# Offsets' taps in four column groups, image 0's first-stage result added in the last sweep, corner rows through two banks and four tiles

## What is computed

```python
x = x + _L0_conv_ref(_gn(x), ...)   # a scan over 4096 tokens and a 3x3 convolution
x = x + _L1_conv_ref(_gn(x), ...)   # four sweeps: down, up, right, left
x = x + _L2_conv_ref(_gn(x), ...)   # column convolution times a gate
x = x + _L3_conv_ref(_gn(x), ...)   # deformable 3x3 convolution, batch norm over all images
```

```python
om = conv3x3(x, offset_w) + offset_b          # 27 channels
samp = corner(y0, x0, ..) + corner(y0, x0 + 1, ..) + corner(y0 + 1, x0, ..) + corner(y0 + 1, x0 + 1, ..)
out = einsum('bckhw,ock->bohw', samp * mask, dcn_w)
```

## Time and profile before

| | us |
|---|---|
| median of three executions | 7023.92 |
| their range | 7022.62 to 7032.38 |
| the profiled execution | 7014.16 |
| its span, first to last instruction | 7012.3 |
| PE busy in the span | 5902.3 (84%) |
| DVE busy | 5302.7 (76%) |
| POOL busy | 4107.6 (59%) |
| ACT busy | 3572.3 (51%) |

### The profile page before, as it was taken

One profiled execution on the slowest core, in us unless ns is written; L12 is line 12 of the kernel. 1 busy time (PEld: TensorE's weight loads), 2 busy tenths in 40 slices (PEclk: granted clock), 3 DMA queues, 4 the chain that ended last, 5 costly groups with the idle time before them and its releaser, 6 DMA issues. The chain is left out here.

```text
span 7012.3 us, 91346 instructions
## 1 busy us (share of the span) xinstructions
PE 5902.3 (84%) x21659; PEld 3273.6 (47%) x21659; DVE 5302.7 (76%) x12723; ACT 3572.3 (51%) x7357; POOL 4107.6 (59%) x3869
## 2 busy tenths in 40 slices
PE   5999999999998999999998877777778787777542
PEld 2444444444447888888885333333333333333221
DVE  6999999999994555566664478787878787777767
ACT  4878878788885531122221345454545454545433
POOL 4999999999991000100000277777777777777773
PEclk9999999999999999999999998989989899999765
DMA  5455444444442000000002478787878787878777
GB/s 193 169 181 184 164 170 171 171 168 169 171 164 83 3 4 0 0 0 0 0 0 67 142 237 247 230 252 223 261 219 266 210 271 211 265 220 251 224 209 288
DMA packets 325492, 1132.55 MB, mean 162 GB/s; under 512 B 58527, under 2 KB 59568, under 8 KB 283952
## 3 DMA queue, kind: packets, MB, share of 16 engines
q0 software_dynamic: 187200, 629.56, 30.3%
q1 hardware_dynamic: 137846, 498.65, 19.7%
HBM read 997.68 MB, written 130.29 MB: 161 GB/s over the span
## 5 line engine op out<-in xcount | busy, mean ns | idle before, releaser
L1255 POOL DMA_INDIRECT d_ring<-corner_table,d_idx_now x2304 | 2210.7, 960 | 925.4 <-issue 848.1
L959 POOL TENSOR_TENSOR X<-X 128x512 f32<-128x512 f32 x1024 | 1288.2, 1274 | 169.3 <-DVE X L997 153.0
L1301 ACT ACTIVATE d_mix<-d_ring,d_w_now 128x128 f32<-128x128 f32 x2304 | 735.5, 390 | 1223.2 <-DMA d_ring<-corner_table,d_idx_now 1151.4
L271 PE MATMUL prop_ps<-prop_parts,prop_w_hi 128*128 128x496 f32 (+2 forms) x4536 | 1143.2, 396 | 0.0
L997 DVE TENSOR_TENSOR_SCAN X<-X,m_pB 128x512 f32<-128x512 f32 x896 | 1135.8, 1273 | 0.0
L853 PE MATMUL m_pY<-X,small 128*128 128x512 f32 x2048 | 1040.5, 605 | 90.1 <-POOL X L959 89.9
L1623 DVE SCALAR_TENSOR_TENSOR d_acc<-d_ring,d_w_now,d_mix 128x128 f32<-128x128 f32 x2304 | 662.9, 355 | 564.2 <-ACT d_mix L1301 543.7
L1449 PE MATMUL d_ps_s<-small,d_mix 128*128 128x128 f32 x2304 | 430.3, 317 | 777.1 <-DVE d_mix L1623 775.5
L271 PEld LDWEIGHTS prop_ps<-prop_parts,prop_w_hi 128*128 128x128 f32 x4536 | 819.1, 189 | 162.3
L1449 PEld LDWEIGHTS d_ps_s<-small,d_mix 128*128 128x128 f32 x2304 | 281.3, 157 | 1276.5 <-DVE d_mix L1623 683.7
L215 ACT ACTIVATE prop_parts<-X 128x256 fp32r (+1 forms) x512 | 276.7, 541 | 1170.8 <-DVE X L292 1170.3
(11 more groups left out here) (229 smaller groups left out, 7568.9 us busy)
## 6 DMA issues: line engine op xcount, KB each, us to landing
X<-c_scratch SPq DMA_DIRECT2D x256, 1024.0 KB, 4.9
corner_table<-d_tT SPq DMA_DIRECT2D x264, 256.0 KB
d_ring<-corner_table,d_idx_now POOLq DMA_INDIRECT x2304
X<-in_x SPq DMA_DIRECT2D x8, 2048.0 KB, 15.2
m_res<-in_x SPq DMA_DIRECT2D x64, 256.0 KB, 4.6
x_scratch<-m_res SPq DMA_DIRECT2D x64, 256.0 KB, 2.1
x_scratch<-X SPq DMA_DIRECT2D x8, 2048.0 KB, 8.6
b_x<-x_scratch POOLq DMA_DIRECT2D x16, 1024.0 KB, 11.8
```

The source lines that it names most:

```text
L271: mm = pe.matmul(ps[s][:, :, :, a:b], w_hi[:, d % 2, k * P:(k + 1) * P], parts[s][:, :, :, PAD + a + k - MID:PAD + b + k - MID], start=Fal ...
L959: pool.tensor_tensor(hc[:, n % NHC, :], h[:, n, :], Cb[:, n, :], ALU.mult).then_inc(s.HC, 1)
L1255: pool.indirect_dma_start(out=ring[:, m % RING, :], out_offset=None, in_=flat, in_offset=bass.IndirectOffsetOnAxis(ap=idx_now[:, c % 2, m: ...
L1301: r0 = act.activation(R[:, k % 3, t, :], ring[:, m % RING, 0:P], ACT.Copy, scale=w_now[:, c % 2, 4 * m:4 * m + 1])
```

## The change

There are three parts.

**Offsets.** The weights of a tap are padded from 27 to 32 columns, and tap `tap` writes partitions `32 * (tap % 4)` to `32 * (tap % 4) + 31` of `ps_a`, so that the nine products are summed in four groups of 32 partitions. ACT copies all 128 partitions (the bias stands in the first 27), and the four turning matmuls take 128 rows and four identities stacked on one another, which sums the groups.

**Image 0's `x1`.** SP loads it in layer 1, whole, into 8 of the 12 tiles of `ring`, which is now allocated there. In the last sweep DVE adds a column of 64 elements of it behind each `lo` of group 0, one column late; the last is added behind the loop. In `add_x1`, image 0 keeps only the statistics. The zeroing of the second table moves to layer 1 too: POOL zeroes the 4 other tiles and issues 17 DMAs from them. In the block of layers 2 and 3, POOL has no `ring` to zero, and SP has eight loads less and one small store more.

**Corner rows.** While nothing is sampled (pass -1), round `m` uses `ps_b` or `ps_s[0]` in turn and one of four tiles, the halves of `tT` and two of `samp`; PE waits for the copy of round `m - 2`, ACT for the store of round `m - 4`. In the other passes all this stays as it was, but the semaphores of the stores are four instead of two.

```diff
@@ layer1 @@
+                sp.dma_start(first_x1[:].rearrange("p h w -> p (h w)"), x1_dram[:, 0:HW]).then_inc(G.first_x1_landed, 16)
...
+                clear = G.ring[0:W + 1, HW // (4 * P):, :]
+                pool.memset(clear.rearrange("p r e -> p (r e)"), 0.0).then_inc(s_zero, 1)
                 weights2.make(pool)
+                pool.wait_ge(s_zero, 2)
+                for x0 in range(0, W + 1, clear.shape[1]):
+                    n = min(clear.shape[1], W + 1 - x0)
+                    pool.dma_start(G.table[1, :, x0:x0 + n, :], clear[:, 0:n, :]).then_inc(G.table_cleared, 16)
...
+                def add_first_x1(t):
+                    dve.wait_ge(s_lo[0], t + (1 + H * 3))
+                    x = line(3, 0, t)[:, 0, :]
+                    dve.tensor_tensor(x, x, first_x1[:, :, t * -1 + (H - 1)], ALU.add).then_inc(s_added, 1)
...
                             rest_of_line(d, t, s)
+                            if s == 0 and d == 3:
+                                add_first_x1(t - 1)
@@ layers2_and_3 @@
-                    for i in range(NCH):
-                        sp.dma_start(first_x1(i), x1_dram[:, CH * i:CH * (i + 1)]).then_inc(s_first[i // 4], 16)
+                    sp.sem_inc(s_add, NCH)
...
-                    pool.memset(ring[:].rearrange("p r e -> p (r e)"), 0.0).then_inc(s_zero, 1)
...
+            def table_tile(s, m):
+                if s.sampling or m % TILES < 2:
+                    return tT[:, m % 2, :]
+                return samp[:, m % 2, :]
+            def table_bank(s, m):
+                return ps_b if s.sampling or m % 2 == 0 else ps_s[0]
...
-                            act.wait_ge(s_tab[m % 2], 16 * IMAGE_STORES[m % 2] * q + 16 * (m // 2))
-                            act.activation(tT[:, m % 2, :], ps_b[:].rearrange("p t c -> p (t c)"), ACT.Copy).then_inc(s_tT, 1)
+                            before = m - (2 if s.sampling else TILES)
+                            if before >= 0:
+                                act.wait_ge(s_tab[before % TILES], 16 * IMAGE_STORES[before % TILES] * q + 16 * (before // TILES + 1))
+                            act.activation(table_tile(s, m), table_bank(s, m)[:].rearrange("p t c -> p (t c)"), ACT.Copy).then_inc(s_tT, 1)
...
-                            act.activation(om_s[:], ps_a[0:NO, :], ACT.Identity, bias=off_b[:, 0:1]).then_inc(s_offs, 1)
+                            act.activation(om_s[:], ps_a[:], ACT.Identity, bias=off_b[:, 0:1]).then_inc(s_offs, 1)
...
-                        after(pe, s_tT, ROUNDS * q + m, 1)
+                        after(pe, s_tT, ROUNDS * q + m, 1 if s.sampling else 2)
...
-                        mm = pe.matmul(ps_a[0:NO, :], off_w[:, tap, :],
+                        quad = tap % QUADS
+                        mm = pe.matmul(ps_a[QUAD * quad:QUAD * (quad + 1), :], off_w[:, tap, :],
                                        xn[:, i % 2, at:at + ROWS * E].rearrange("p (h w) -> p h w", w=E)[:, :, 0:W],
-                                       start=(tap == 0), stop=(tap == TAPS - 1))
+                                       start=(tap < QUADS), stop=(tap + QUADS >= TAPS))
...
-                                turned = pe.matmul(ps_om[:, t, :], om_s[:, t * P:(t + 1) * P], G.ident[0:NO, 0:NO],
+                                turned = pe.matmul(ps_om[:, t, :], om_s[:, t * P:(t + 1) * P], off_w[:, TAPS, 0:NO],
...
-                        if isinstance(q, int) and q == 0:
-                            dve.wait_ge(s_first[i // 4], 64)
-                        else:
+                        x = XF[:, bass.ds(CH * gA, CH)]
+                        if not (isinstance(q, int) and q == 0):
                             dve.wait_ge(s_x1, 16 * gA + (16 - 16 * NCH))
-                        apart(dve, s_passed_dve)
-                        x = XF[:, bass.ds(CH * gA, CH)]
-                        dve.tensor_tensor(x, x, first_x1(i) if isinstance(q, int) and q == 0 else x1[:], ALU.add).then_inc(s_add, 1)
+                            apart(dve, s_passed_dve)
+                            dve.tensor_tensor(x, x, x1[:], ALU.add).then_inc(s_add, 1)
                         after(dve, s_add, gA)
```

More of the change, by code:

```diff
@@ L1025, in layers2_and_3 @@
     NO = 3 * TAPS
-    NCLEAR = -(-E // RING)
+    QUAD, QUADS = 32, P // 32
+    NCLEAR = -(-E // (RING - HW // (4 * P)))
     ROUNDS = E * E // P
-    IMAGE_STORES = (ROUNDS // 2 + 2, ROUNDS // 2)
+    TILES = 4
+    IMAGE_STORES = [len(range(i, ROUNDS, TILES)) for i in range(TILES)]
+    IMAGE_STORES[(ROUNDS - 1) % TILES] += 1
     assert E * E == ROUNDS * P + 1 and ROUNDS % 2 == 1
@@ L1066, in sem @@
             return ctx.enter_context(nc.semaphore(name))
-        table = nc.dram_tensor("corner_table", (2, E, E, 4 * P), F32).ap()
+        table = G.table
         base = sb("d_base", [P, 2, NCH, NG])
-        off_w = sb("d_off_w", [P, TAPS, NO])
-        off_b = sb("d_off_b", [NO, 1])
+        off_w = sb("d_off_w", [P, TAPS + 1, QUAD])
+        off_b = sb("d_off_b", [P, 1])
         dcn_w = sb("d_dcn_w", [P, TAPS, P])
@@ L1118, in layers2_and_3 @@
             s_tT = sem("d_table_tile_out")
-            s_clear = sem("d_second_table_cleared")
-            s_tab = [sem(f"d_table_stored{i}") for i in range(2)]
+            s_tab = [sem(f"d_table_stored{i}") for i in range(TILES)]
             s_math = sem("d_index_steps")
@@ L1193, in _ @@
                         sp.dma_start(dst, G.d[n]).then_inc(s_const, 16)
-                    sp.wait_ge(s_zero, 5)
-                    sp.dma_start(table[0, H, W:E, P:4 * P], ring[0:1, 0, 0:3 * P]).then_inc(s_border, 16)
-                    sp.wait_ge(s_border, 16)
+                    sp.wait_ge(s_zero, 4)
+                    sp.wait_ge(G.table_cleared, 16 * NCLEAR)
+                    for a in range(2):
+                        sp.dma_start(table[a, H, W:E, P:4 * P], xn[0:1, 0, 0:3 * P]).then_inc(s_border, 16)
                     sp.wait_ge(s_const, 16 * 7)
@@ L1208, in image @@
                                      G.X[:, q, :]).then_inc(s_x3, 16)
-                        if s.first:
-                            sp.wait_ge(s_clear, 16 * NCLEAR)
                         if s.adding:
@@ L1218, in image @@
                             apart(sp, s_passed)
-                            sp.dma_start(flat[P * m:P * (m + 1), :], tT[:, m % 2, :]).then_inc(s_tab[m % 2], 16)
-                        sp.dma_start(flat[E * E - 1:E * E, 0:P], tT[P - 1:P, (ROUNDS - 1) % 2, P:2 * P]).then_inc(s_tab[(ROUNDS - 1) % 2], 16)
+                            sp.dma_start(flat[P * m:P * (m + 1), :], table_tile(s, m)).then_inc(s_tab[m % TILES], 16)
+                        sp.dma_start(flat[E * E - 1:E * E, 0:P], table_tile(s, ROUNDS - 1)[P - 1:P, P:2 * P]).then_inc(s_tab[(ROUNDS - 1) % TILES], 16)
                     passes(sp, image)
-                    for i in range(2):
+                    for i in range(TILES):
                         sp.wait_ge(s_tab[i], 16 * IMAGE_STORES[i] * B)
+                    sp.wait_ge(s_border, 32)
                     sp.wait_ge(s_x3, 16 * B)
@@ L1229, in _ @@
                     pool.memset(zero[:], 0.0).then_inc(s_zero, 1)
-                    pool.memset(ring[:].rearrange("p r e -> p (r e)"), 0.0).then_inc(s_zero, 1)
                     pool.memset(xn[:].rearrange("p a f -> p (a f)"), 0.0).then_inc(s_zero, 1)
                     pool.memset(tb[:], 0.0).then_inc(s_zero, 1)
-                    pool.wait_ge(s_zero, 5)
                     flat = table.rearrange("a y x e -> (a y x) e")
-                    for x0 in range(0, E, RING):
-                        n = min(RING, E - x0)
-                        pool.dma_start(table[1, :, x0:x0 + n, :], ring[0:E, 0:n, :]).then_inc(s_clear, 16)
                     def image(s):
@@ L1241, in image @@
                         if s.first:
-                            pool.wait_ge(s_border, 16)
-                            pool.wait_ge(s_clear, 16 * NCLEAR)
-                        for i in range(2):
+                            pool.wait_ge(s_border, 32)
+                            pool.wait_ge(G.table_cleared, 16 * NCLEAR)
+                        for i in range(TILES):
                             pool.wait_ge(s_tab[i], 16 * IMAGE_STORES[i] * s.p + 16 * IMAGE_STORES[i])
@@ L1764, in build_program @@
             if n == "L1":
+                G.ring = sb("d_ring", [P, G.RING, 4 * P])
+                G.first_x1_landed = ctx.enter_context(nc.semaphore("first_x1_landed"))
+                G.table_cleared = ctx.enter_context(nc.semaphore("second_table_cleared"))
+                G.table = nc.dram_tensor("corner_table", (2, W + 1, W + 1, 4 * P), F32).ap()
                 group_norm_scales(nc, ctx, G, summed=True)
```

37 lines of the change are left out of this document (21 added, 16 removed).

## The result

| | before | changed |
|---|---|---|
| median of 6 runs each, same chip | 7023.52 us (7022.55 to 7032.38) | 6988.87 us (6987.91 to 6994.3) |
| ratio, 95% interval | 1 | 0.9949 (0.9936 to 0.9962) |
| profiled execution, its span | 7014.16, 7012.3 | 6988.72, 6986.8 |

A forecast was written before the change was run, and what follows sets the result against it. POOL's gathers were taken to pace sampling, PE and DVE together the sweeps, PE alone the table stage. The terms -13.3 + 11.0 + 0.4 - 30 - 3 gave -35 us, a median of 6989 us, range 6968 to 7019.

The forecast's parts named there:

- Image 0's x1, the gain: Between last sweep and normalisation: statistics begin at SP's first DMA instead of waiting for x1, -13.3 us.
- Its cost: Last sweep: 63 column adds on DVE's chain, +11.0 us, bounds 0 and 22.
- Offsets' taps: Table stage: taps in different column groups overlap, 1.06 us a slot of two or three, -30 us over eight chunks.
- Banks and tiles: Table stage: second bank and four tiles are worth 0 by themselves but keep the taps' gain.
- Sampling: Images' sampling: PE saves time that POOL mostly does not wait for, -3 us, between +5 and -20.
- A dearer sweep with half the gain of the taps: Last sweep and table stage: add costs +22, taps give -15, 7017 us in all; chance 16%.
- Groups that do not overlap: Table stage: column groups do not run side by side, +1 in all, 7025 us; chance 12%.
- PE's clock: Sampling: relieved PE drops to half clock in some slots, slower by over 0.2% from 46 us; chance 6%.
- the gentler case: Last sweep and sampling: add costs only 3, sampling gains 12, -52 in all, 6972 us; chance 14%.

The follow-up runs named there:

- e3: Changed kernel with image 0's x1 added behind the sweeps from the tile where it lies, no add in the last sweep; 6989.41 us.
- e6: Changed kernel with the column add moved one place, into DVE's pause while ACT rounds; sweep 397.5 us, ratio to before 0.9947.
- e10: Changed kernel with a second small DVE instruction of the same size behind each column add; one run, last sweep 419.5 us instead of 404.4.
- e1: Changed kernel with the offsets' taps in one group of 27 columns again, everywhere; 7015.48 us, ratio to before 0.9989.
- e4: Changed kernel with corner rows through one PSUM bank and two tiles again; 6984.36 us, ratio to before 0.9945.
- e5: Changed kernel with column groups only for image 0's chunks ahead of sampling, one group beside sampling; 6983.81 us, ratio to before 0.9940.
- a0: The changed kernel run again, unaltered, later on another chip; 7799.72 us, ratio to before 0.9955.
- e8: e6 with a chunk's nine taps dealt to its four slots as 3, 3, 3, 0 instead of 3, 2, 2, 2; ratio to before 0.9927.
- e9: e8 with ACT's copy of the offsets' sum one slot earlier; ratio to before 0.9914.
- e11: e9 with the nine taps dealt as 4, 4, 1, 0 instead of 3, 3, 3, 0; ratio to before 0.9911.
- e12: e9 with corner rows through one PSUM bank and two tiles again, as in e4; ratio to before 0.9938.
- b0: The kernel before run again, unaltered, later on another chip; 7838.7 us, one run.

## Why the prediction came out right

**Image 0's x1, the gain:** -13.3 and +0.4 for the last add behind the loop forecast, -13.1 measured for both. The start at SP's first DMA and the 5.1 us behind it came as written, and that DMA comes 5.5 us behind the last copy instead of 5.1, by the last add.

**Its cost:** +11.0 forecast, +6.9 measured. The mechanism was right (e3, e6, e10 show it from three sides); the term was over-sized. I took 0.308 us for the add and 0.24 in the chain, with 0.06 of slack. The add lasts 0.27 and puts in 0.19, with 0.08 of slack; the step's 0.109 x 63 = 6.9. The Trainium skill's rule (SBUF — State Buffer, two separate sides), by which each access on a new line of 16 bytes pays, led to 353 ns: at 274 ns the add pays something over the 225 that I worked out for a contiguous one, but far less than my reading of that rule made of it.

**Offsets' taps:** -30 forecast, -34.7 measured. The nearest row gave the right 1.06 us for the records, but the next transposes start before the last record ends, 0.98 us behind the first. So the taps of a chunk save 3 x 0.85 + 1.68 = 4.23 (the slot of three lasted 2.67 before, not my 2.69), and the 0.15 that I gave back for ACT's copy is not there (PE waits 0.29, for 0.27 before); measured 4.32. The rest is a part that I did not count: the eight turning matmuls hold PE 0.91 us with 128 rows, where they held it 1.00 with 27, and the transposes behind them 0.56 instead of 0.59. For three groups the Trainium skill (TensorE: Matmul & The Clock Gate, Part 3) gives 2.38 times; this case's slots show 2.67 / 0.99 = 2.7 for three. The forecast of a chunk was 8.0 us, measured 7.54.

**Banks and tiles:** "By itself this part is 0; it keeps the taps' gain" was right: nothing in e1, 3.0 of the 34.7 us with fast taps.

**Sampling:** -3 forecast, +12.3 in the profiled pair, outside my +5 to -20. The term is not confirmed. The medians give -34.7 in all where the stages give -40.9, which leaves about +6 for all the rest, less than the interval of the ratio (some 9 us either way). The same count gives +7 for e3 and -3 for e4, with groups beside sampling, and -3 for e1 and -1 for e5, without; and in the later runs, all with groups, +6 for a0, 0 for e6, -14 for e8, +1 for e9, -2 for e11 and +5 for e12, where the intervals are wider. So it is somewhere near nothing, and the direction stays open.

**The rivals.** A dearer sweep with half the gain of the taps (+22 and -15): both halves wrong, with +6.9 and -34.7. Groups that do not overlap: shown wrong by e1 and e11. PE's clock: its first step came (0.91 to 0.88, and back in e5), its price did not: no 46 us, and in e4 images 0 to 6 were quicker at 0.88 than in e5 at 0.91. Of the gentler case the sweep came halfway (6.9, between its 3 and my 11), and sampling did not gain the 12. That the total of -35 was met is in part luck: up to the first gather the kernel gained 9 us more than my terms (4 in the sweep, 5 in the taps), and behind it 9 less than the -3 (about +6 by the medians).

## What to carry to other kernels

An instruction added to a loop whose engines share the pace costs what it puts into the chain less the slack, so look for the pause that another engine's work leaves on the same engine; two lines of code apart, this add cost 6.9 us or nothing. When the bound of a stage becomes faster, what stands in order behind it decides next: here one ACT copy behind another held back 7.5 of the next 11.1 us, and a second bank with two more tiles was worth nothing, 3.0 and 9.7 us at chunks of 11.9, 7.5 and 6.1 us. The sum of an engine's waits is not what they cost: follow each to the engine that sets the pace. Compare by stages that repeat within 0.7 us where the whole time scatters by more than the effect.

## What the runs showed of the hardware that was not expected

- Matmuls of 32 columns in different column groups, with different moving data and all 128 rows, ran beside one another without a visible price: two, three or four taps of 512 columns in fp32 took 1.06 us by the records, starts 7 ns apart. A lone tap in e11 held PE until the next transposes for 0.98 us, a slot of four for 1.00, so a slot of four does the work of four in the time of one.
- An add of 128x64 with two strided inputs and a strided output took 0.27 us, between the 0.233 of a contiguous one of 72 elements and my 0.308. The next instruction started 0.18 us behind it.
- The gathers' speed differed between the first runs and the later ones on other chips: 3307 to 3369 us for images 0 to 6 instead of 2582 to 2594, while everything ahead of them agreed. The median interval between gathers was 1.26 us in b0 and 1.25 in the first trace of before. The difference lies in few long intervals: in b0 185 of the 2016 were over 2 us and 52 over 8, in the first trace 10 and none. What held those transfers, and whether it goes with the chip or the time, the traces don't show.
